# Expert gates turned in 32x32 blocks on VectorE, and expert products over six PSUM banks

## The reference

```python
scores = xf @ Wr.T                              # (1024, 64)
top_vals, top_idx = jax.lax.top_k(scores, 16)
gates = jax.nn.softmax(top_vals, axis=-1)
G = zeros((N, 64)).at[rows, top_idx].set(gates) # one row of gates per token, 48 of 64 are zero
h = jnp.einsum('nd,krd->nkr', xf, A)            # 64 experts x 16 ranks = 1024 rows
out = jnp.einsum('nkr,kdr->nd', h * G[:, :, None], B) * 2.0
x = x + out
```

## Time and profile before

| | |
|---|---|
| median of 3 runs | 354.89 us (354.57 to 354.99) |
| the profiled execution | 354.69 us, of which the profile's span is 353.0 us |
| TensorE busy in the span | 349.5 us (99%), granted clock 1.000 |
| VectorE, ScalarE, GpSimd busy | 202.2 us, 144.1 us, 78.0 us |

### The profile page before, as it was taken

The page is one execution under the profiler, slowest core; times in us unless marked ns, Lnnn a source line. Parts: engine busy times, 40 slices in busy tenths (PEclk is TensorE's granted clock), DMA queues, the critical chain, the costliest instruction groups (busy, mean ns, idle before and its releaser), DMA issues.

```text
span 353.0 us, 4621 instructions
## 1 busy us (share of the span) xinstructions
PE 349.5 (99%) x1682; PEld 294.4 (83%) x1682; DVE 202.2 (57%) x302; ACT 144.1 (41%) x196; POOL 78.0 (22%) x86
## 2 busy tenths in 40 slices
PE   8999999999999999999999999999999999999997
PEld 8899888888888888888888898888888888888885
DVE  3788755334533453685674565879888878501102
ACT  5577544422442243545464471566352443201100
POOL 2361657863340004000000000000041154002200
PEclk9999999999999999999999999999999999999999
DMA  7943343232120054297219019010052022101011
GB/s 202 323 126 144 114 138 112 78 104 77 52 80 0 0 177 130 79 395 291 59 35 306 3 22 417 38 52 11 0 177 62 0 61 69 51 32 59 30 61 59
DMA packets 14802, 37.31 MB, mean 106 GB/s; under 512 B 2272, under 2 KB 4224, under 8 KB 13504
## 3 DMA queue, kind: packets, MB, share of 16 engines
q1 hardware_dynamic: 11920, 31.18, 25.9%
q0 software_dynamic: 2432, 5.57, 5.5%
q10 hardware_dynamic: 432, 0.33, 0.3%
HBM read 34.97 MB, written 2.10 MB: 105 GB/s over the span
## 4 chain that ended last, share of the span: by engine, by line
PE 99%; DVE 0%; issue 0%
PE ps L1157 29%; PE ps L1158 29%; PE ps L1159 29%; PE ps L1179 3%; PE ps L1309 3%; PE ps L1399 1%; PE ps L1386 1%; PE ps L1194 1%; PE ps L1187 1%; PE ps L1198 1%; PE ps L1202 1%; PE ps L1234 1%; PE ps L1408 0%; PE ps L1417 0%; DVE x L1149 0%
## 5 line engine op out<-in xcount | busy, mean ns | idle before, releaser
L1158 PE MATMUL ps<-x_hl,w_hl 128*128 128x512 f32 x144 | 56.2, 390 | 0.0
L1157 PE MATMUL ps<-x_hl,w_hl 128*128 128x512 f32 x144 | 56.2, 390 | 0.0
L1159 PE MATMUL ps<-x_hl,w_hl 128*128 128x512 f32 x144 | 56.1, 389 | 0.0
L462 POOL TENSOR_TENSOR am_hl<-am_raw,am_hl 128x512 fp32r<-128x512 f32 x8 | 11.0, 1387 | 137.4 <-ACT am_hl L479 137.4
L418 POOL DMA_INDIRECT b_raw<-b_gu,row_of x32 | 32.1, 1003 | 27.7 <-DVE b_st L780 19.6
L800 DVE TENSOR_TENSOR glu<-glu,ps 128x512 f32<-128x512 f32 (+1 forms) x22 | 14.9, 683 | 38.8 <-ACT glu L511 26.0
L1159 PEld LDWEIGHTS ps<-x_hl,w_hl 128*128 128x128 f32 x144 | 27.1, 188 | 5.7
L511 ACT ACTIVATE glu<-ps 128x512 f32<-128x512 f32 (+1 forms) x22 | 12.8, 588 | 46.0 <-PE ps L1179 45.8
L1157 PEld LDWEIGHTS ps<-x_hl,w_hl 128*128 128x128 f32 x144 | 27.1, 188 | 5.4
L1158 PEld LDWEIGHTS ps<-x_hl,w_hl 128*128 128x128 f32 x144 | 27.1, 188 | 5.2
L1158 PE MATMUL ps<-act,wd_hl 128*128 128x512 f32 x80 | 31.2, 390 | 0.0
(11 more groups left out here) (151 smaller groups left out, 729.0 us busy)
## 6 DMA issues: line engine op xcount, KB each, us to landing
wc_raw<-mask_w SPq DMA_DIRECT2D x8, 1024.0 KB, 7.0
w_raw<-w_gu SPq DMA_DIRECT2D x8, 512.0 KB, 3.3
wd_raw<-w_dn SPq DMA_DIRECT2D x10, 256.0 KB, 2.7
w_raw<-w_t SPq DMA_DIRECT2D x2, 1024.0 KB, 7.3
x<-x_blocks SPq DMA_DIRECT2D x2, 1024.0 KB, 6.3
am_raw<-a_moe SPq DMA_DIRECT2D x8, 256.0 KB, 2.8
bm_raw<-b_moe SPq DMA_DIRECT2D x4, 512.0 KB, 3.6
x_raw<-x_blocks SPq DMA_DIRECT2D x7, 256.0 KB, 6.7
```

The costliest lines, as they stand in the source:

```text
L462: nc.gpsimd.tensor_tensor(am_hl[:, j % AM_SLOTS, 1], am_raw[:, j % 2], am_hl[:, j % AM_SLOTS, 0].bitcast(F32), ALU.subtract).then_inc(am_l ...
L1157: nc.tensor.matmul(out, w_high, m_high, start=start, stop=False)
L1158: nc.tensor.matmul(out, w_high, m_low, start=False, stop=False)
L1159: return nc.tensor.matmul(out, w_low, m_high, start=False, stop=stop)
```

## The change

The gates are no longer turned by TensorE. VectorE scales them in one instruction (gate_tok, 128 tokens by 4 groups by 64 experts) where four did it before. It then turns them itself, with eight transposes for each half. Each takes 32 partitions of tokens and 4 x 32 columns, and turns them as four blocks of 32x32 into 32 partitions of gate_x; the loop over e picks the output's 32 partitions, the loop over q the input's. ScalarE's copy now takes partitions 0 to 63 of gate_x to 64 to 127. Bank 6 is so no longer needed for the turned gates, and the expert products rotate over banks 0, 1, 2, 3, 6, 7 instead of 0 to 3. A product's wait on its bank moves from four products back to six. The first `combine` asks for both gate copies.

```diff
+BLOCK = 32
+H_BANKS = (0, 1, 2, 3, 6, 7)
...
-        gate2 = at("gate2", [P, 4, 2, EXPERTS], F32, R_ACT + 54 * KB)
+        gate_tok = at("gate_tok", [P, 4, EXPERTS], F32, R_ACT + 54 * KB)
...
             def gate_copy(s):
-                act_e.wait_ge(gate_tr, s + 1)
-                copy(gate_x[:, s], ps[:, 6]).then_inc(late_banks_free, 2)
+                act_e.wait_ge(gate_turned, s + 1)
+                copy(gate_x[EXPERTS:P, s], gate_x[0:EXPERTS, s]).then_inc(late_banks_free, 2)
...
                 step(nc.vector.reciprocal(gate_inv[:], gate_sum[:]))
-                if s:
-                    dve.wait_ge(gate_tr, s)
-                for t in range(4):
-                    last = nc.vector.tensor_scalar(
-                        gate2[:, t], left1[:, t].unsqueeze(1).broadcast_to([P, 2, EXPERTS]),
-                        gate_inv[:, t:t + 1], MOE_SCALE, ALU.mult, ALU.mult)
-                last.then_inc(gate_done, 1)
+                step(nc.vector.scalar_tensor_tensor(gate_tok[:], left1[:], MOE_SCALE,
+                                                    gate_inv[:].unsqueeze(2).broadcast_to([P, 4, EXPERTS]),
+                                                    ALU.mult, ALU.mult))
+                for e in range(0, EXPERTS, BLOCK):
+                    turned = gate_x[e:e + BLOCK, s].rearrange("p (t q n) -> p t q n", t=4, n=BLOCK)
+                    for q in range(P // BLOCK):
+                        last = nc.vector.transpose(turned[:, :, q],
+                                                   gate_tok[q * BLOCK:q * BLOCK + BLOCK, :, e:e + BLOCK])
+                last.then_inc(gate_turned, 1)
...
-                nc.vector.tensor_tensor(hg_raw[:, n % 2], ps[:, n % 4], gate_x[:, s],
+                nc.vector.tensor_tensor(hg_raw[:, n % 2], ps[:, H_BANKS[n % len(H_BANKS)]], gate_x[:, s],
...
-            def turn_gates(s):
-                pe.wait_ge(gate_done, s + 1)
-                if s:
-                    pe.wait_ge(late_banks_free, 2)
-                for t in range(4):
-                    last = nc.tensor.transpose(ps[:, 6, t * P:t * P + P],
-                                               gate2[:, t].rearrange("p c e -> p (c e)"), ident)
-                last.then_inc(gate_tr, 1)
-
             def experts(n, part=range(KD)):
...
-                if n >= 4:
-                    pe.wait_ge(hg_mul, n - 3)
+                if n >= len(H_BANKS):
+                    pe.wait_ge(hg_mul, n - len(H_BANKS) + 1)
...
-            turn_gates(0)
             pe.wait_ge(ct_lo, BATCH)
...
-            turn_gates(1)
...
-                    pe.wait_ge(late_banks_free, 2 * o + s + 1)
+                    pe.wait_ge(late_banks_free, max(4, 2 * o + s + 1))
```

More of the change, by code:

```diff
@@ L233, in build @@
         s_ready, s_copied, score_ready = sem("s_ready"), sem("s_copied"), sem("score_ready")
-        top_step, shifted, exp_done, gate_done = sem("top_step"), sem("shifted"), sem("exp_done"), sem("gate_done")
-        gate_tr, late_banks_free = sem("gate_tr"), sem("late_banks_free")
+        top_step, shifted, exp_done = sem("top_step"), sem("shifted"), sem("exp_done")
+        gate_turned, late_banks_free = sem("gate_turned"), sem("late_banks_free")
         am_hi, am_lo, h_ready, hg_mul, hg_hi, hg_lo = (sem("am_hi"), sem("am_lo"), sem("h_ready"), sem("hg_mul"),
@@ L1424, in experts @@
                 pe.wait_ge(am_lo, j + 1)
-                if n >= 4:
-                    pe.wait_ge(hg_mul, n - 3)
+                if n >= len(H_BANKS):
+                    pe.wait_ge(hg_mul, n - len(H_BANKS) + 1)
                 for k in part:
-                    last = mm3(ps[:, n % 4], am_hl[:, j % AM_SLOTS, 0, k], am_hl[:, j % AM_SLOTS, 1, k],
+                    last = mm3(ps[:, H_BANKS[n % len(H_BANKS)]], am_hl[:, j % AM_SLOTS, 0, k], am_hl[:, j % AM_SLOTS, 1, k],
                                c_hl[:, 0, k, halves(s)], c_hl[:, 1, k, halves(s)], k == 0, k == KD - 1)
```

## The result

The changed kernel takes 355.64 us (median of 11 runs, 355.36 to 356.23) against 354.89 us (354.57 to 355.25). The ratio is 1.0024, with a 95% interval from 1.0014 to 1.0033: slower by 0.24%, where I had forecast no change (354.85 us). The time lies in the stated range, but the kernel did get slower, which I had not forecast.

The account below looks back on a forecast made before the run. TensorE, busy 349.5 of 353.0 us, was taken as the bound. Its 0.82 us saving against a 0.75 us wait at product 8 gave -0.07 us; the forecast was 354.85 us, no change, range 353.95 to 356.2.

Parts of the forecast that it names:

- So TensorE waits from 283.98 to 284.68 and about 0.05 for the semaphore: TensorE at product 8, reached at 283.98 without the turns, waits for GpSimd's am_low(4), ending at 284.68: 0.75 us.
- The saving: TensorE no longer does its two turns of the gates, 0.37 and 0.45 us: 0.82 us, 0.23% of the time.
- The first turn: VectorE's turns for the first half begin at 266.40, after one scaling of 0.44 us and a 0.24 hold by GpSimd.
- The length of a turn: VectorE, from one turn to the next: 0.29 + 0.01 = 0.30 us, 2.4 us for eight; bounds 0.20 and 0.43.
- ScalarE's three copies: hg_high(3), gate_copy(1) and am_high(4) ahead of am_low(4): gate_copy(1) about 0.53 us after hg_high(3), 0.50 between the next two.
- The end of the wait: TensorE's start of product 8 after am_low(4) ends: about 0.05 us allowed for the semaphore.
- a bank is not what is late: Expert products on TensorE: a later gate of half 1 is covered by six banks, and something else is late before a bank.
- Nothing by themselves: What the six banks bring: no time, since TensorE never waited for a bank before.
- A second wait: Rival, chance 0.13: product 11's tile comes later than its 0.2 us spare allow, adding 0.3 to 0.8 us: 355.2 to 355.6.
- overlap of the turns: Rival, chance 0.20: VectorE's turns overlap or are shorter, 0.20 us each, so the full 0.82 us is gained: 354.07 us.
- turns of 0.43: Upper bound for a VectorE turn, as long as 256 columns moved on 32 partitions: sum +2.0 us, 356.9 us.
- the slower rival: Rival, chance 0.13: VectorE's turns take much longer, each 0.01 us of a turn costing 0.16 us; decides from 0.349 us.

## Why the prediction was wrong

The mechanism was the one that happened: TensorE saves its turns, one wait takes their place, at product 8, for am_low(4), behind sixteen turns that do not overlap. What failed is the size of that wait, in the step "So TensorE waits from 283.98 to 284.68 and about 0.05 for the semaphore": 0.75 us, where 1.46 were lost. With a saving of 0.82 and a cost of 0.75 the sum was a small difference, and the 0.7 us by which the wait came short decided the sign. Term by term, times of the changed profile taken 0.31 earlier:

- The saving: 0.82 predicted, 0.88 measured from turn_scores(1) to product 8. Right.
- The first turn: 266.40 predicted, 266.37 measured. Right, GpSimd's hold included: the scaling took 0.74 the first time, not 0.42.
- The length of a turn: 0.30 predicted, 0.313 measured (0.301 each, and 0.013 to the next). It enters sixteen times, 0.21 us; with the small steps around the two sets hg_low(2) began at 280.57 instead of 280.33, 0.24 us of the error. A part of this was arithmetic: 0.424 less 128 columns at 1.0 ns is 0.296, which I put down as 0.29. The lack of overlap was right, and two experiments show it. The Trainium skill's rule in "VectorE: DVE Perf Modes", section "Two Vector instructions with no wait between them", names the change of the input's and of the output's quadrant; the experiment with the input's partitions held and the one with the output's changed agree with it for each (1.77 and 2.50 us for eight). The 311 ns that the Trainium skill gives in "VectorE: DVE Perf Modes", section "The three transpose paths", are for 128x128 in bf16; a turn of 32x128 in fp32 took 301 ns here, and 258 where it was not held. With 311 ns my sum would have ended at +0.27, not at the +0.25 that I wrote.
- ScalarE's three copies: I took 0.53 and 0.50 between their starts, since ScalarE's instructions overlapped in the earlier trace rows. They stood 0.66 apart: 0.29 us. This is the largest single miss. I had counted on VectorE that a change of partitions ends the overlap, and did not ask the same of ScalarE, whose copy the change moves from partitions 0 to 63 to 64 to 127. The profile of the kernel before had the answer, in the pair of t_st at 24.79.
- The end of the wait: 0.07 instead of 0.05 for the semaphore, and 0.09 for a slower first matmul after it, which I had left out although shows a 0.31 after each interruption. TensorE also came 0.06 earlier than I had it.

Together 0.24 + 0.29 + 0.02 + 0.09 + 0.06 = 0.70, and 0.75 + 0.70 is the 1.46 measured, but for rounding.

The other steps. The claim that in the changed kernel a bank is not what is late holds with six banks: the wait is released by am_hl. "Nothing by themselves" for the banks is right in the time and wrong in its reason: with four, product 7 waits first. A second wait at products 9 to 11 did not come; by the timelines products 9 and 10 had 1.0 and 0.9 us to spare, not 0.9 and 0.7. Of the rivals, overlap of the turns was not what happened, though the experiment with the input's partitions held shows that it would have brought the gain; turns of 0.43 were not either. The price that the slower rival gave, 0.16 us for every 0.01 of a turn, holds for the wait: 16 more turns made it 5.0 us longer.

## What to carry to other kernels

Work taken from the engine that sets the end becomes time only if what it then reaches earlier is ready earlier; follow the list of the engine that takes the work over, and the lists behind it, down to the first thing that the bound engine needs. Here three instructions in another order on ScalarE turned a loss of 0.24% into a gain of 0.30%, and the six banks only counted once that was done. Where an instruction writes from another group of partitions than the one before it, count it from start to end, on ScalarE as on VectorE; on VectorE the same was seen for the partitions that it reads. When a forecast is the difference of two nearly equal terms, its sign is open until each link of the wait has a row.

## What was not expected

A wait of TensorE can cost more than itself: one of 6.2 us was followed by twelve matmuls in 5.10 us instead of 2.72, most of them at a granted clock of 0.50, so another 2.4 us; after one of 1.2 us the clock stayed at 1.00. And ScalarE copies of 512 columns start 0.66 us apart instead of 0.52 when one of them writes from partition 64 on and the others from 0.
